# Last attention's loop: the weighted values of a group of tiles issued behind the next group's sums, not in steps between them

## The chip, the cores and the metric

The kernel runs on one core of a Trainium2 chip. The metric is the device time of one execution in microseconds (us); less is better. The engines of the core run side by side, each through its own list of instructions, and meet only at semaphores: TensorE (PE; PEld is its loading of weights), VectorE (DVE), ScalarE (ACT), GpSimd (POOL) and SyncE (SP), which issues the DMAs.

## The reference, cut to what matters

The program is a stack of four layers, each an attention to a context and a feed-forward part, with gated residuals. The change is in the attention of the last layer: 1024 tokens attend to 2048 context rows with 16 heads of width 16. Queries, keys, values and probabilities are rounded to a grid of integers (fake quantization):

```python
q = _fq_sym(q, axis=-1); k = _fq_sym(k, axis=-1); v = _fq_sym(v, axis=2)
attn = jnp.einsum('bhqd,bhkd->bhqk', q, k)
attn = jax.nn.softmax(attn.astype(jnp.float32), axis=-1)
attn = _fq_unsigned(attn, axis=-1)     # s = max / 255; round(attn / s) * s
out = jnp.einsum('bhqk,bhkd->bhqd', attn, v)
```

The largest probability of a row has the exponent 0 after the maximum is taken off, so a rounded probability is the rounded 255 * exp(logit - maximum), and the sum that divides it is that of the exponentials before rounding.

## The kernel before

`layer3_attention` lays out its loop by hand. One head at a time, it needs the maximum of each query's logits before it can form exponentials, so the logits are formed twice: first with the queries on the partitions (`scores`, L2717), from which VectorE takes the maxima (L2891), then with the keys on the partitions and the maximum as three more rows of the contraction (`logits`, L2733), 128 keys by 512 queries in a PSUM bank, of which ScalarE takes the exponentials (L2819, `a_exps`).

The loop runs over steps `s`, 16 for a head (`PER`), and each engine has its own copy of the loop. A step of TensorE issues:

- `scores(s)`: two matmuls, for 128 queries and half the keys. They wait for `ring_free`, that is, for VectorE's maxima of the step before the last: the ring has two places of two banks.
- `logits(m, 0)` and `logits(m, 1)`: the two tiles of pair `m`, `LAG` = 25 steps behind the scores. Each waits until ScalarE has emptied one of three banks.
- work on the exponentials, four steps later (`FILL_LAG`). Four tiles, two pairs, are a group. A chunk is half the queries of a head: 8 steps, numbered `k` = 0 to 7, and 4 groups (`n`, the chunk, and `k` come from `fill_at`). `sums(n, i)` (L2742) adds up the four tiles of group `i` over the keys; it waits for the exponentials. `weighted(n, i)` (L2753) multiplies the rounded tiles by the values; it waits for the rounding of the group's two pairs. Both put their four tiles next to each other into four strips of 32 columns of the array, and into one bank (`OUT`). `sums` reads four-byte exponentials, `weighted` two-byte rounded ones.
- once a head `rows` (L2724), which turns the maxima, and once a head `turn_heads` (L2764), which turns the outcome of a head back.

In the kernel before, sums stand in the steps with odd `k` and the weighted values of groups 0 to 2 in the even step after, between the two logits; those of group 3 come in step 7 behind the second logits.

The rounding of a pair is GpSimd's: L2648 adds a large constant (`a_xn_t` by its older name), L2651 takes it off and writes the two-byte `a_stack`. For every fourth pair, and for all from pair 233 on, VectorE does it in one instruction (L2926, `round_pair`), after the maxima of step `m` + 27. The rounded pairs have six buffers (`PAIRS`), so that a rounding of pair `m` waits for the weighted values of the group that held pair `m` - 6. The exponentials have nine pairs of buffers. GpSimd also splits a head's maxima into three parts (L2656 to L2662), once a head. ScalarE copies the bank `OUT` away after the last group of a chunk (`keep_out`, L2825); the sums of the next chunk wait for that.

No DMA depends on the order of these steps but those of the maxima (L2620), three a head, issued by SyncE.

Of the kernel before, what the change touches and what calls it, by code (L numbers as in the profile page):

```python
# [315 lines left out]
def at_least(eng, sem, value):  # L316

    if isinstance(value, int) and value <= 0:
        return
    eng.wait_ge(sem, value)  # L320
# [2171 lines left out]
def layer3_attention(core):  # L2492
# [10 lines left out]
    with ExitStack() as ctx:  # L2503
# [49 lines left out]
        GROUPS = KT // TILES_PER  # L2553
        STEPS = 2 * GROUPS
# [3 lines left out]
        def fill_at(s):  # L2558

            n, k = divmod(s - LAG - FILL_LAG, STEPS)  # L2560
            return (n, k) if 0 <= n < CHUNKS else (None, None)
# [19 lines left out]
        def rows_slot(s):  # L2581

            h, k = divmod(s - PER - ROWS_LAG, PER)
            return h if k == 0 and 0 <= h < H else None

        def pair_at(s):

            return s - LAG if 0 <= s - LAG < H * PER else None
# [5 lines left out]
        def rounded_by_vector(m):  # L2594

            return sum(by_vector(k) for k in range(m))

        def rounded_by_pool(m):

            return m - rounded_by_vector(m)  # L2600

        with nc.Block() as block:
# [68 lines left out]
            def _(pe):  # L2671
# [39 lines left out]
                def scores(s):  # L2711
                    h, (t, half) = s // PER, divmod(s % PER, 2)
                    n = ring_use["scores", s]
                    if n >= 2:
                        pe.wait_ge(ring_free, n - 1)
                    for c in range(2):
                        mm = pe.matmul(ring(("scores", s))[:, c * BANK:(c + 1) * BANK], qs[0:KS, h * TOK + t * P:h * TOK + (t + 1) * P],  # L2717
                                       ks[0:KS, h * CTX + (2 * half + c) * BANK:h * CTX + (2 * half + c + 1) * BANK], start=True, stop=True)
                    mm.then_inc(ring_full, 1)

                def rows(h):
                    pe.wait_ge(ring_free, ring_use["rows", h] - 1)
                    pe.wait_ge(parts_ready, h + 1)
                    pe.transpose(ring(("rows", h)).bitcast(BF16)[0:3 * NT, 0:P], max_parts[:, h, :, :].rearrange("p s t -> p (s t)"),  # L2724
                                 core.ident_bf[:, :]).then_inc(ring_full, 1)

                def logits(m, u):
                    h, (c, j) = m // PER, divmod(m % PER, KT // 2)
                    if m % PER == 0 and u == 0:
                        pe.wait_ge(ROWS_IN[h % 2], 48 * (h // 2 + 1))  # L2730
                    n, key = 2 * m + u, 2 * j + u
                    at_least(pe, exp_ready, n - LOGIT_BANKS + 1)
                    pe.matmul(core.bank(LOGITS + n % LOGIT_BANKS), ks[0:KM, h * CTX + key * P:h * CTX + (key + 1) * P],  # L2733
                              qs[0:KM, h * TOK + c * QC:h * TOK + (c + 1) * QC], start=True, stop=True).then_inc(logits_full, 1)

                def sums(n, i):
                    g = n * GROUPS + i
                    if i == 0:
                        at_least(pe, out_kept, n)
                    pe.wait_ge(exp_ready, TILES_PER * (g + 1))  # L2740
                    for u in range(TILES_PER):
                        mm = pe.matmul(core.bank(OUT)[32 * u:32 * u + W, :], one_row[:, :], exps[:, (TILES_PER * g + u) % UNITS, :],  # L2742
                                       start=(i == 0), stop=False, skip_group_check=True)
                    mm.then_inc(sums_done, 1)

                def weighted(n, i):
                    g = n * GROUPS + i
                    if g == 0:
                        pe.wait_ge(v_ready, 1)
                    at_least(pe, probs_by_pool, rounded_by_pool(2 * (g + 1)))  # L2750
                    at_least(pe, probs_by_vector, rounded_by_vector(2 * (g + 1)))
                    for u in range(TILES_PER):
                        mm = pe.matmul(core.bank(OUT)[32 * u:32 * u + W, :], v_int[:, TILES_PER * i + u, n // CH, :],  # L2753
                                       probs[:, (2 * g + u // 2) % PAIRS, u % 2 * QC:(u % 2 + 1) * QC],
                                       start=False, stop=(i == GROUPS - 1), skip_group_check=True)
                    mm.then_inc(weighted_done, 1)

                def turn_heads(h):
                    pe.wait_ge(ring_free, ring_use["heads", h] - 1)
                    pe.wait_ge(out_kept, CH * (h + 1))  # L2760
                    tiles = QC // P
                    for c in range(CH):
                        for t in range(tiles):
                            mm = pe.matmul(ring(("heads", h))[:, (c * tiles + t) * W:(c * tiles + t + 1) * W],  # L2764
                                           outs[(CH * h + c) % OUTS][:, t * P:(t + 1) * P], select[:, :], start=True, stop=True)
                    mm.then_inc(ring_full, 1)

                for s in range(SLOT_COUNT):
                    n, k = fill_at(s)
                    if s < H * PER:  # L2770
                        scores(s)
                    if pair_at(s) is not None:
                        logits(pair_at(s), 0)
                    if n is not None and k % 2 == 1:
                        sums(n, k // 2)
                    if n is not None and k % 2 == 0 and k > 0:
                        weighted(n, k // 2 - 1)
                    if pair_at(s) is not None:
                        logits(pair_at(s), 1)
                    if n is not None and k == STEPS - 1:  # L2780
                        weighted(n, GROUPS - 1)
                    if rows_slot(s) is not None:
                        rows(rows_slot(s))
                    if s in TURN_OF:
                        turn_heads(TURN_OF[s])
# [691 lines left out]
```

## Time and profile before

| | |
|---|---|
| median of 3 runs | 3300.67 us (3296.85 to 3310.09) |
| the profiled execution's own time | 3297.79 us |
| its span, first to last instruction | 3296.1 us |
| TensorE busy over the span | 2811.4 us (85%) |
| VectorE / ScalarE / GpSimd busy | 2056.2 / 1520.8 / 828.0 us |
| first exponential of the loop starts | 2418.6 us |
| last exponential of the loop starts | 2865.4 us |

The profiled execution is one of its own, beside the three timed ones. Times in the rows below are microseconds from the start of the span. The loop that is changed fills some 450 us of it. Matmuls are pipelined: the recorded duration of one is longer than the distance to the next, so costs on TensorE are read from start to start.

### The profile page before, as it was taken

To read this page: it belongs to the slowest core of one execution; us is meant where nothing else is said; L and a number is where in the kernel's file an instruction comes from. 1 tells how busy PE (TensorE), PEld (TensorE's weight loads), DVE (VectorE), ACT (ScalarE), POOL (GpSimd) and SP (SyncE) were. 2 spreads that over 40 slices of the span, in tenths; PEclk is the share of its full clock that TensorE was granted. 3 is DMA by queue.
4 is the path that set the end of the run, shared out by engine and by line. 5 is a ranking of instruction groups with operands and counts; after the bars stand their busy time and mean duration, and the time that the engine had idled before them with its cause. 6 is when DMAs were issued, how large, how long until landed. Compare 5 with 4: busy or idle time off the path is not lost. (4 is left out here: it accounts for less than half of the span.)

```text
span 3296.1 us, 47304 instructions
## 1 busy us (share of the span) xinstructions
PE 2811.4 (85%) x15010; PEld 1820.7 (55%) x15010; DVE 2056.2 (62%) x4872; ACT 1520.8 (46%) x3119; POOL 828.0 (25%) x1217
## 2 busy tenths in 40 slices
PE   6887995888899999837999999935689999957898
PEld 4334663777677777615777777724323233334676
DVE  5775336777666666575444444477988888577332
ACT  3452225677666777542222222212347777634221
POOL 0011004444422212010000000031089999402100
PEclk9898997999999999957999999967789999977899
DMA  1002003000000000003000000001000000020000
GB/s 58 1 2 87 1 0 128 14 1 14 14 1 7 8 1 1 1 34 128 1 1 1 0 0 0 0 20 38 8 1 1 1 2 1 1 97 2 1 1 13
DMA packets 37912, 56.98 MB, mean 17 GB/s; under 512 B 6400, under 2 KB 25792, under 8 KB 36416
## 3 DMA queue, kind: packets, MB, share of 16 engines
q1 hardware_dynamic: 37696, 54.35, 4.9%
q8 instruction: 105, 1.72, 0.2%
q14 instruction: 111, 0.91, 0.1%
HBM read 52.99 MB, written 1.05 MB: 16 GB/s over the span
## 5 line engine op out<-in xcount | busy, mean ns | idle before, releaser
L2819 ACT ACTIVATE a_exps<-psum,a_ln 128x512 f32<-128x512 f32 x512 | 333.8, 687 | 147.7 <-PE psum L2733 147.3
L2891 DVE TENSOR_REDUCE a_half_max<-psum 128x1 f32<-128x1024 f32 x256 | 305.2, 1215 | 48.4 <-PE psum L2717 46.6
L1903 DVE TENSOR_REDUCE a_neg_max<-psum 128x2 f32<-128x512 f32 (+1 forms) x128 | 122.5, 957 | 172.0 <-PE psum L1606 169.1
L1556 POOL TENSOR_TENSOR a_head_rstd<-a_head_var,neg_half 128x4 f32<-128x4 f32 x112 | 114.4, 1021 | 394.6 <-DVE a_head_var L1897 214.0
L1626 PE MATMUL psum<-a_probs_t,a_vals 128*128 128x256 f32 x768 | 191.8, 386 | 15.9 <-ACT a_probs_t L1783 15.9
L2651 POOL TENSOR_SCALAR a_stack<-a_xn_t 128x1024 bf16<-128x1024 f32 x175 | 192.9, 1102 | 27.3 <-POOL a_xn_t L2648 26.6
L847 DVE SCALAR_TENSOR_TENSOR f_silu<-f_silu,psum 128x352 f32<-128x352 f32 (+2 forms) x88 | 50.4, 572 | 229.6 <-ACT f_silu L820 229.5
L2648 POOL TENSOR_SCALAR a_xn_t<-a_exps 128x1024 f32<-128x1024 f32 x175 | 191.1, 1092 | 9.1 <-ACT a_exps L2819 9.1
L1606 PE MATMUL psum<-a_k_t,a_q_t 128*128 128x256 f32 (+1 forms) x512 | 190.3, 495 | 0.0
L2733 PE MATMUL psum<-a_qs,a_ks 99*128 99x512 bf16 x512 | 190.0, 387 | 0.1
L1097 DVE TENSOR_REDUCE a_neg_max<-psum 128x2 f32<-128x1024 f32 x64 | 78.4, 1225 | 177.2 <-PE psum L1092 177.2
L2717 PE MATMUL psum<-a_ks,a_qs 96*128 96x512 bf16 x512 | 165.3, 407 | 27.0 <-DVE a_half_max L2891 21.2
L1751 ACT ACTIVATE a_normed<-psum,a_head_bias,a_head_scale 128x128 f32<-128x128 f32 x448 | 168.9, 465 | 40.3 <-POOL a_head_bias L1561 39.3
L1791 ACT ACTIVATE a_probs<-psum,a_neg_max 128x256 f32<-128x256 f32 (+1 forms) x256 | 146.8, 581 | 42.7 <-DVE a_neg_max L1903 42.5
L1626 PEld LDWEIGHTS psum<-a_probs_t,a_vals 128*128 128x128 f32 x768 | 139.8, 191 | 43.4 <-ACT a_probs_t L1783 27.6
L1783 ACT COPY a_probs_t<-psum 128x512 f32<-128x512 f32 x192 | 112.6, 586 | 99.7 <-PE psum L1615 97.4
L1104 ACT ACTIVATE a_probs<-psum,a_neg_max 128x512 f32<-128x512 f32 x128 | 86.7, 682 | 153.3 <-DVE a_neg_max L1097 153.3
L1250 PEld LDWEIGHTS psum<-a_w_v,a_ctx_b 128*128 128x128 f32 x1024 | 124.3, 192 | 31.8 <-issue 30.0
L2733 PEld LDWEIGHTS psum<-a_qs,a_ks 99*128 99x128 bf16 x512 | 48.7, 97 | 164.8 <-ACT a_exps L2819 130.4
L781 PE MATMUL psum<-f_w_silu,f_tile_t 128*128 128x352 f32 (+2 forms) x352 | 136.3, 510 | 3.3 <-issue 2.6
L1638 PE MATMUL psum<-a_w_parts,a_cat 128*128 128x256 f32 x512 | 102.4, 323 | 42.7 <-DVE a_cat L1342 42.7
L805 PE MATMUL psum<-f_w_down,f_hid_t 128*128 128x256 f32 (+1 forms) x576 | 138.7, 380 | 0.0
(485 smaller groups left out, 6415.0 us busy)
## 6 DMA issues: line engine op xcount, KB each, us to landing
a_w_raw<-in_L_xattn_wproj_dram SPq DMA_DIRECT2D x8, 512.0 KB, 3.8
f_w_silu<-in_L_ffn_gate_dram SPq DMA_DIRECT2D x1, 2112.0 KB, 9.3
f_w_mul<-in_L_ffn_up_dram SPq DMA_DIRECT2D x1, 2112.0 KB, 13.9
a_probs<-in_ctx_t_dram SPq DMA_DIRECT2D x4, 512.0 KB, 5.4
f_w_silu<-in_L_ffn_Wu_dram SPq DMA_DIRECT2D x1, 2048.0 KB, 7.9
f_w_mul<-in_L_ffn_Wg_dram SPq DMA_DIRECT2D x1, 2048.0 KB, 12.5
f_w_down<-in_L_ffn_Wd_dram SPq DMA_DIRECT2D x1, 2048.0 KB, 17.5
a_q_raw<-in_L_xattn_wq_dram SPq DMA_DIRECT2D x4, 512.0 KB, 6.8
```

The costliest lines, as they stand in the source:

```text
L781: mm = pe.matmul(core.bank(bank)[:, 0:w], self.tile_t[:, tr, k, :], weights[:, k, first:first + w], start=(k == 0), stop=(k == DK - 1))
L805: mm = pe.matmul(core.bank(6 + tr2)[:, 0:D], self.hid_t[0:w, r, i, :], self.w_down[0:w, base + i, :], start=(c2 == 0 and i == 0), stop=(c2 ...
L1606: mm = pe.matmul(core.bank(SCORES + t)[:, 0:keys], q_t[:, quad % 2, h, t * P:(t + 1) * P], k_t[:, quad % 2, h // 2, 0:keys], start=True, s ...
L1626: mm = pe.matmul(core.bank(OUT)[:, 0:S], vals[:, quad % 2, j, (h // 2) * P:(h // 2 + 1) * P], probs_t[:, g % 2, j, :], start=(j == 0), sto ...
L1751: last = act.activation(normed[:, i % 2, j * P:(j + 1) * P], bank[:, j * P:(j + 1) * P], ACT.Identity, bias=head_bias[:, i % 4, j:j + 1], ...
L1791: last = act.activation(probs[:, g % 2, t, 0:keys], core.bank(SCORES + t)[:, 0:keys], ACT.Exp, bias=neg_max[:, g % 2, t:t + 1], accum_out= ...
L2648: g.tensor_scalar(up, exps[:, first:first + 2, :].rearrange("p u n -> p (u n)"), 1.0, ROUND, ALU.mult, ALU.add).then_inc(lifted_ready, 1)
L2651: g.tensor_scalar(probs[:, m % PAIRS, :], up, -ROUND, 1.0, ALU.add, ALU.mult).then_inc(probs_by_pool, 1)
L2717: mm = pe.matmul(ring(("scores", s))[:, c * BANK:(c + 1) * BANK], qs[0:KS, h * TOK + t * P:h * TOK + (t + 1) * P], ks[0:KS, h * CTX + (2 * ...
L2733: pe.matmul(core.bank(LOGITS + n % LOGIT_BANKS), ks[0:KM, h * CTX + key * P:h * CTX + (key + 1) * P], qs[0:KM, h * TOK + c * QC:h * TOK + ...
L2819: act.activation(exps[:, n % UNITS, :], core.bank(LOGITS + n % LOGIT_BANKS), ACT.Exp, bias=ln255[:, :]).then_inc(exp_ready, 1)
L2891: v.tensor_reduce(half_max[:, h, t, half:half + 1], ring(("scores", s)), AX.X, ALU.max, negate=True).then_inc(ring_free, 1)
```

## The change

Weighted values no longer have steps of their own. Those of group `i` - 1 are issued in the odd step of group `i`, behind its sums and ahead of the second logits; in the last step of a chunk (`k` = 7) those of groups 2 and 3 both follow the sums of group 3, also ahead of the second logits. The loops of the other engines, the waits and the buffers stay.

```diff
                     if n is not None and k % 2 == 1:
                         sums(n, k // 2)
-                    if n is not None and k % 2 == 0 and k > 0:
-                        weighted(n, k // 2 - 1)
+                        if k > 1:
+                            weighted(n, k // 2 - 1)
+                        if k == STEPS - 1:
+                            weighted(n, GROUPS - 1)
                     if pair_at(s) is not None:
                         logits(pair_at(s), 1)
-                    if n is not None and k == STEPS - 1:
-                        weighted(n, GROUPS - 1)
                     if rows_slot(s) is not None:
                         rows(rows_slot(s))
```

## Rows read from the trace of the kernel before

**Rows 1.** Busy time in two stretches: from:to, length, each engine (instructions), clock, DMA.
```profile
2443.00:2837.00 394.00, 384.18 (x2422) 119.18 (x2421) 333.24 (x328) 300.48 (x470) 364.76 (x386) 1.00 0.01 1
2841.00:2866.00 25.00, 24.83 (x173) 7.00 (x175) 13.26 (x21) 23.33 (x39) 0.00 (x0) 1.00 0.00 1
```

**Rows 2.** GpSimd's groups, 2443 to 2837 us: busy, mean ns, idle before.
```profile
L2651 POOL TENSOR_SCALAR a_stack<-a_xn_t 128x1024 bf16<-128x1024 f32 x165 | 182.1, 1104 | 26.2 <-POOL a_xn_t L2648 25.8 <-PE psum L2753 0.3
L2648 POOL TENSOR_SCALAR a_xn_t<-a_exps 128x1024 f32<-128x1024 f32 x165 | 180.2, 1092 | 0.0
```

**Rows 3.** GpSimd's timeline, one instruction of a head and of the next: start, us.
```profile
2603.61 0.19 POOL L2656 CAST a_max_parts<-a_neg_max 128x8 bf16<-128x8 f32 x1
...
2632.31 0.19 POOL L2656 CAST a_max_parts<-a_neg_max 128x8 bf16<-128x8 f32 x1
```

**Rows 4.** Waits of the weight loads, 2443 to 2837 us: total, times, longest.
```profile
PEld psum L2753 <- POOL a_stack L2651: 5.3, 19, 0.4
```

**Rows 5.** Timeline at the end of an even chunk.
```profile
2608.24 1.04 POOL L2651 TENSOR_SCALAR a_stack<-a_xn_t 128x1024 bf16<-128x1024 f32 x1 [0.15 <-POOL a_xn_t L2648]
...
2609.42 0.10 PEld L2753 LDWEIGHTS psum<-a_stack,a_v_int 128*17 128x17 bf16 x4 [0.23 <-POOL a_stack L2651]
```

**Rows 6.** Timeline of two steps of TensorE, and a later rounding of GpSimd.
```profile
2616.32 1.05 PE L2742 MATMUL psum<-a_exps,a_one_row 128*17 128x512 f32 x8
...
2617.30 0.39 PE L2733 MATMUL psum<-a_qs,a_ks 99*128 99x512 bf16 x1
...
2617.53 0.60 PE L2717 MATMUL psum<-a_ks,a_qs 96*128 96x512 bf16 x2
...
2617.97 0.38 PE L2733 MATMUL psum<-a_qs,a_ks 99*128 99x512 bf16 x1
...
2618.28 0.39 PE L2753 MATMUL psum<-a_stack,a_v_int 128*17 128x512 bf16 x4
...
2618.60 0.39 PE L2733 MATMUL psum<-a_qs,a_ks 99*128 99x512 bf16 x1
...
2619.57 1.05 PE L2742 MATMUL psum<-a_exps,a_one_row 128*17 128x512 f32 x8
...
2624.17 1.04 POOL L2651 TENSOR_SCALAR a_stack<-a_xn_t 128x1024 bf16<-128x1024 f32 x1 [0.15 <-POOL a_xn_t L2648]
```

**Rows 7.** Timeline of TensorE at the loop's end, where no logits are left.
```profile
2865.32 0.39 PE L2753 MATMUL psum<-a_stack,a_v_int 128*17 128x512 bf16 x4
...
2865.54 1.03 PE L2742 MATMUL psum<-a_exps,a_one_row 128*17 128x512 f32 x8
...
2866.40 0.39 PE L2753 MATMUL psum<-a_stack,a_v_int 128*17 128x512 bf16 x4
```

**Rows 8.** Timeline in the loop's tail.
```profile
2841.21 8.12 ACT L2819 ACTIVATE a_exps<-psum,a_ln 128x512 f32<-128x512 f32 x13 [0.62 <-PE psum L2733]
...
2841.95 0.10 PEld L2733 LDWEIGHTS psum<-a_qs,a_ks 99*128 99x128 bf16 x1 [0.21 <-ACT a_exps L2819]
...
2843.26 0.11 PEld L2733 LDWEIGHTS psum<-a_qs,a_ks 99*128 99x128 bf16 x2 [0.85 <-ACT a_exps L2819]
```

**Rows 9.** Timeline: two roundings of VectorE and GpSimd's instructions beside them.
```profile
2604.92 1.25 DVE L2926 TENSOR_SCALAR a_stack<-a_exps 128x1024 bf16<-128x1024 f32 x1
...
2605.78 1.28 POOL L2651 TENSOR_SCALAR a_stack<-a_xn_t 128x1024 bf16<-128x1024 f32 x1 [0.15 <-POOL a_xn_t L2648]
...
2627.37 0.68 DVE L2926 TENSOR_SCALAR a_stack<-a_exps 128x1024 bf16<-128x1024 f32 x1
...
2627.39 1.57 POOL L2648 TENSOR_SCALAR a_xn_t<-a_exps 128x1024 f32<-128x1024 f32 x1
```

**Rows 10.** Busy time in two stretches of other parts of the program.
```profile
140.00:160.00 20.00, 18.32 (x102) 7.56 (x102) 13.70 (x35) 10.48 (x11) 0.40 (x1) 0.68 0.00 1
200.00:220.00 20.00, 17.19 (x143) 7.07 (x147) 14.95 (x37) 10.33 (x12) 2.36 (x6) 1.00 0.01 2
```

## The prediction

> **What bounds the loop now.** I read the page for the size of things, then one table of busy time over the loop's steady stretch and its tail, then GpSimd's groups of instructions and the waits of that stretch, and last the timeline of single steps.
>
> The change touches only the loop of the last attention. In 2443 to 2837 us TensorE is busy 384.2 of 394.0 us at a granted clock of 1.00, GpSimd 364.8, VectorE 333.2, ScalarE 300.5 [rows 1]. That looks like a TensorE bound, and the change looks like a gift to it. But busy share does not say which engine waits. GpSimd's two operations for a pair of tiles have 165 runs each, and the only idle time in front of them is 26.2 us in front of L2651, 0.15 us for each pair, put down to GpSimd's own L2648 just before (0.3 us of it to TensorE); in front of L2648 it is 0.0 [rows 2]. So GpSimd never waits for exponentials and never for a free buffer: it is saturated by a dependency chain of its own. Its pace is the loop's: its split of one head's maxima starts at 2603.61 and at 2632.31, 28.70 us apart, and a head is 16 steps [rows 3]. TensorE on its side waits for GpSimd little: 5.3 us in 19 waits of the weight load of the weighted values [rows 4]. At the end of an even chunk (a chunk is half a head's queries, 8 steps) the rounding that the fourth group needs ends at 2608.24 + 1.04 = 2609.28, and its weighted values start at 2609.42 [rows 5]. TensorE is therefore level with GpSimd: 0.14 us later, and it would start to wait. I read this as a loop paced by GpSimd with TensorE hard behind it.
>
> **What the change does to TensorE.** It adds and removes no instruction and no DMA. Weighted values of groups 0 to 2 of a chunk move from the even step to the odd step after it, behind the sums; those of group 3 stay in the last step, but go in front of the second logits.
>
> Prices from single steps [rows 6], start to start; two steps take 3.25 us, 2616.32 to 2619.57. Apart: the first logits of the even step at 2617.97, weighted at 2618.28, second logits at 2618.60, so 0.63 us from logits to logits where the plain spacing is 0.22 (two score matmuls from 2617.53, the logits behind them at 2617.97): the weighted values cost 0.41. Sums to logits is 0.98 (2616.32 to 2617.30). Joined does not occur in the loop's middle, but the loop's end has it, where no logits are left between: weighted to sums is 0.22 (2865.32 to 2865.54), sums to weighted 0.86 (2865.54 to 2866.40) [rows 7]. So sums, weighted, logits takes 0.86 + 0.32 = 1.18 in place of 0.98: 0.20 added. Net 0.41 - 0.20 = 0.21 us saved for each of the 4 x 32 = 128 groups, 27 us of TensorE's time in all. Bounds: 0 if the four-byte sums and the two-byte weighted values change over as dearly as logits and weighted do (0.41), 0.21 by rows 7, the nearest; I take 0.21. The Trainium skill, TensorEngine Tiling (Array Packing), Key Properties, has the reason: a change of the array's tiling mode drains TensorE, while changing between tiles of one mode does not. The rows agree (0.31 and 0.32 against 0.22); by that rule alone two drains in two steps go, and where TensorE sets the pace the time would come down by what they cost.
>
> **What hides it.** I cost the saving at nothing as long as GpSimd sets the pace. About 116 of the 128 groups lie ahead of GpSimd's last pair, 116 x 0.21 = 24 us; uncovered, that would be the gain. Instead TensorE arrives 8 x 0.21 = 1.7 us earlier per head at a rounding that comes no sooner, and the 19 short waits become longer ones.
>
> Behind the new wait stand the second logits and the next scores. ScalarE waits for the logits, VectorE for the scores. Neither is late for GpSimd: when TensorE waits for pair 6 of a chunk, logits up to four or five pairs further have been issued, so GpSimd keeps its supply.
>
> The moved groups also give GpSimd's buffers back one step (1.6 us) later: a rounding needs the weighted values of the group six pairs back. The weighted values at 2618.28 free what the L2651 at 2624.17 writes [rows 6]: 5.9 us early, 4.3 after the change. No stall, so nothing.
>
> **The part that isn't hidden: the tail.** After GpSimd's last pair (it has no instruction in 2841 to 2866 [rows 1]) VectorE rounds alone and there are no scores; ScalarE sets the pace, 13 exponentials in 8.12 us, 0.62 each, back to back [rows 8]. The chain there has no slack that I can see: the first logits of an odd step wait for a bank (2841.95, 0.21 us put down to the exponentials), the second come 1.31 us later, at 2843.26, behind the sums, with 0.39 us to their end, 1.70 in all, while the three logits banks hold 3 x 0.62 = 1.86 us of work for ScalarE, less hand-over [rows 8]. With weighted values between, the 1.31 becomes 1.51 in steps 3 and 5 of a chunk and 1.71 in step 7 (two groups). Chunks 29 and 30 have four such placings each, chunk 31 one before the logits end, and the last step of chunk 28 is delayed by one: 10 x 0.20 = +2.0 us. Bounds: 0 if the banks hide it, 10 x 0.41 = +4.1 if the joint is dear. I take +2.0, by rows 7.
>
> **GpSimd's own pace** can still change. A VectorE rounding that falls beside GpSimd's work stretches it: with one starting at 2604.92, which took 1.25, the L2651 at 2605.78 took 1.28 in place of 1.04; with one at 2627.37, which took 0.68, the L2648 at 2627.39 took 1.57 [rows 9]. So one rounding costs GpSimd 0.24 or 0.53, by where it arrives. Over the stretch that is 165 x (1.104 - 1.044) + 165 x (1.092 - 1.044) = 17.8 us [rows 2], taking 1.044 for an undisturbed run of either (the 1.04 of rows 5). The change moves TensorE and so VectorE's arrivals. Four roundings a head, 394 / 28.70 = 13.7 heads, 55 roundings: between none that costs (-17.8) and all at 0.53 (29.2 - 17.8 = +11.4). Going through one head, most arrivals hang on GpSimd themselves (TensorE waits for it at chunk ends, VectorE finishes behind it), so I take 0 change and keep both ends. The Trainium skill, SBUF — State Buffer, the section on SBUF's two sides, tells of a port pair that VectorE and GpSimd hold as an exclusive lock for a whole instruction. The rows agree in kind; by that rule each rounding could block GpSimd for its whole 0.68, 55 x 0.68 = 37.4, an estimate of +20 us at most, which would be a slower kernel.
>
> **Sum.** Profiled execution 3297.79 us (span 3296.1, so 1.7 around it): 0 for the steady loop, +2.0 for the tail: 3299.8. The median of the three runs, 3300.67, lies 2.9 above the profiled one; so I predict 3303 us.
>
> **Rivals.**
> *A: TensorE is the bound after all.* For it: 97.5% busy, few waits [rows 1, 4]. Against: GpSimd's idle time is all its own [rows 2], and TensorE cannot run ahead of the rounding. It would give 3300.67 - 24 + 2 = 3279. Chance 0.05.
> *B: VectorE's roundings fall otherwise* and change GpSimd's pace, as costed above: 3285 to 3314. Chance 0.18, of which 0.01 beyond either bound of 16.5 us.
> *C (slower): the clock.* TensorE waits more, its busy share falls from 97.5% to some 360 of 394, 91%, in pieces of a us at each chunk's end. In 140 to 160 us, with 18.32 of 20 busy, the granted clock was 0.68; in 200 to 220, with 17.19, it was 1.00 [rows 10]. So a share of 91% decides nothing alone, and the waits would be short. If the clock fell to its lower level (1.2 of 2.4 GHz), a head's 28 us of TensorE would take up to 28 more: from 0.6 of one head in sixteen on, the kernel is slower by over 0.5%; one head gives about 3330. Chance 0.05.
> *D: the joint saves nothing* (0.41, the upper bound): the loop is hidden as well, the tail pays 4.1: 3305. Chance 0.04.
>
> My forecast has 0.68. Within 0.5% (16.5 us, about what a measurement of this kernel tells from no change): 0.68 + 0.16 + 0.04 = 0.88; faster: A and a part of B, 0.06; slower: C and a part of B, 0.06. The range holds the forecast with its tail's bounds (3300.7 to 3304.8), the spread of single runs around their median (-4 to +9), and most of B: 3293 to 3315.
>
> **What would show it.** Right: GpSimd's groups keep their count and have no idle time but their own; its split returns after 28.7 us; waits of weighted values on GpSimd grow from 5.3 to some 20 to 28 us; sums to weighted 0.86, weighted to logits 0.32; in the tail ScalarE's run of 13 breaks up with gaps of 0.2 us. Wrong: a head shorter than 28.4 us (A, or B to the good), longer than 29 (B), a granted clock under 1.00 in the stretch (C), or GpSimd waiting for weighted values (the 4.3 us of cover misjudged).

## The result and the profile after

The changed kernel took 3312.8 us (median of 20 runs), the kernel before 3302.5 in 20 runs of its own: a ratio of 1.0030, 95% interval 1.0022 to 1.0037, some 10 us slower. That is inside the bound of 0.5% and inside the predicted range, but not the +2 us that the sum gave. (One of these twenty runs, at 5793.9 us, and a few of the experiments' were disturbed and are left out of the ratios.)

The loop alone accounts for it: from the first exponential to the start of the last weighted values it took 448.9 us before (2418.6 to 2867.5) and 458.6 after (2422.1 to 2880.7), +9.7. The profiled execution's span is 14.2 longer (3310.3 against 3296.1); 3.5 us of that had passed before the loop and 1.0 come after it, in code that is the same.

What the change does to TensorE is as priced. Two steps of the changed kernel, timeline of TensorE:

```profile
2593.06 1.05 PE L2742 MATMUL psum<-a_exps,a_one_row 128*17 128x512 f32 x8
2593.93 0.40 PE L2753 MATMUL psum<-a_stack,a_v_int 128*17 128x512 bf16 x4
2594.27 0.39 PE L2733 MATMUL psum<-a_qs,a_ks 99*128 99x512 bf16 x1
...
2596.11 1.05 PE L2742 MATMUL psum<-a_exps,a_one_row 128*17 128x512 f32 x8
```

Sums to weighted 0.87, weighted to logits 0.34, and 3.05 us from sums to sums where [rows 6] have 3.25: 0.20 saved for a group. TensorE's busy time in the steady stretch fell from 384.2 us to 370.9. The two stretches of [rows 1] after, then GpSimd's groups of [rows 2]:

```profile
2443.00:2837.00 394.00, 370.93 (x2411) 126.05 (x2413) 320.13 (x326) 288.18 (x467) 364.15 (x377) 0.98 0.01 1
2841.00:2866.00 25.00, 19.75 (x127) 6.28 (x126) 9.55 (x16) 17.35 (x30) 7.63 (x11) 0.86 0.00 1
```
```profile
L2648 POOL TENSOR_SCALAR a_xn_t<-a_exps 128x1024 f32<-128x1024 f32 x163 | 180.1, 1105 | 1.2 <-ACT a_exps L2819 1.2
L2651 POOL TENSOR_SCALAR a_stack<-a_xn_t 128x1024 bf16<-128x1024 f32 x162 | 178.4, 1101 | 25.7 <-POOL a_xn_t L2648 22.6 <-PE psum L2753 2.9
L2656 POOL CAST a_max_parts<-a_neg_max 128x8 bf16<-128x8 f32 x13 | 5.5, 424 | 0.0
```

GpSimd is still saturated: it has one wait of 1.2 us for exponentials, and the 0.15 us ahead of each L2651 remain. (The 2.9 us put down to TensorE are part of those: the weighted values that these roundings needed had started at least 1.8 us before.) But it does 162 and 163 roundings in the time in which it did 165. Its L2648 went from 1092 to 1105 ns in the mean, and the small cast at the head of the split from some 190 to 424. The heads differ now: the split returns after 28.6 and 29.6 us in turn, where it was 28.7 each time. All its 175 roundings took 419.7 us before and 425.9 after, first start to last end. GpSimd's groups over the whole loop (2405 to 2860 us), before, then after; 9.1 us of the idle time ahead of L2648 stand before the first of them:

```profile
L2651 POOL TENSOR_SCALAR a_stack<-a_xn_t 128x1024 bf16<-128x1024 f32 x175 | 192.9, 1102 | 27.3 <-POOL a_xn_t L2648 26.6 <-PE psum L2753 0.3
L2648 POOL TENSOR_SCALAR a_xn_t<-a_exps 128x1024 f32<-128x1024 f32 x175 | 191.1, 1092 | 9.1 <-ACT a_exps L2819 9.1
L2656 POOL CAST a_max_parts<-a_neg_max 128x8 bf16<-128x8 f32 x16 | 3.0, 189 | 0.0
```
```profile
L2648 POOL TENSOR_SCALAR a_xn_t<-a_exps 128x1024 f32<-128x1024 f32 x175 | 193.1, 1104 | 10.3 <-ACT a_exps L2819 10.3
L2651 POOL TENSOR_SCALAR a_stack<-a_xn_t 128x1024 bf16<-128x1024 f32 x175 | 193.0, 1103 | 27.3 <-POOL a_xn_t L2648 23.5 <-PE psum L2753 3.3
L2656 POOL CAST a_max_parts<-a_neg_max 128x8 bf16<-128x8 f32 x16 | 6.1, 380 | 0.0
```

The three were busy 387.0 us before and 392.2 after, +5.2; with the 1.2 of waiting that is 6.4, about the 6.2 that the stretch grew by.

Where TensorE now waits, of the matmuls and of the weight loads, 2443 to 2837 us:

```profile
PE psum L2724 <- POOL a_max_parts L2662: 16.1, 13, 2.8
PE psum L2717 <- DVE a_half_max L2891: 6.6, 11, 0.8
```
```profile
PEld psum L2753 <- POOL a_stack L2651: 18.2, 39, 0.7
```

The waits for roundings grew from 5.3 us [rows 4] to 18.2, close to what was foreseen; the first line of the matmuls is a wait that the prediction didn't have: once a head, `rows` waits for GpSimd's split, up to 2.8 us.

### The profile page after: what moved, and what is told of

The parts are those of the page before. It is cut to its first block and busy times, and to the rows that moved or that the text cites. A ratio compares the mean times of both kernels' runs of the same rounds, so it can differ in the third digit from the quotient of the medians.

```text
span 3310.3 us, 47302 instructions
## 1 busy us (share of the span) xinstructions
PE 2810.9 (85%) x15008; PEld 1833.3 (55%) x15010; DVE 2041.9 (62%) x4872; ACT 1510.8 (46%) x3119; POOL 834.9 (25%) x1217
## 3 DMA queue, kind: packets, MB, share of 16 engines
HBM read 52.99 MB, written 1.05 MB: 16 GB/s over the span
## 5 line engine op out<-in xcount | busy, mean ns | idle before, releaser
L2819 ACT ACTIVATE a_exps<-psum,a_ln 128x512 f32<-128x512 f32 x512 | 323.7, 689 | 167.9 <-PE psum L2733 167.9
L2651 POOL TENSOR_SCALAR a_stack<-a_xn_t 128x1024 bf16<-128x1024 f32 x175 | 193.0, 1103 | 27.3 <-POOL a_xn_t L2648 23.5
L2648 POOL TENSOR_SCALAR a_xn_t<-a_exps 128x1024 f32<-128x1024 f32 x175 | 193.1, 1104 | 10.3 <-ACT a_exps L2819 10.3
L2733 PE MATMUL psum<-a_qs,a_ks 99*128 99x512 bf16 x512 | 176.5, 390 | 3.1 <-ACT a_exps L2819 3.1
L1626 PEld LDWEIGHTS psum<-a_probs_t,a_vals 128*128 128x128 f32 x768 | 139.6, 191 | 44.4 <-ACT a_probs_t L1783 28.7
L2742 PE MATMUL psum<-a_exps,a_one_row 128*17 128x512 f32 x1024 | 140.8, 623 | 0.1
```

The costliest lines, as they stand in the source:

```text
L1626: mm = pe.matmul(core.bank(OUT)[:, 0:S], vals[:, quad % 2, j, (h // 2) * P:(h // 2 + 1) * P], probs_t[:, g % 2, j, :], start=(j == 0), sto ...
L2648: g.tensor_scalar(up, exps[:, first:first + 2, :].rearrange("p u n -> p (u n)"), 1.0, ROUND, ALU.mult, ALU.add).then_inc(lifted_ready, 1)
L2651: g.tensor_scalar(probs[:, m % PAIRS, :], up, -ROUND, 1.0, ALU.add, ALU.mult).then_inc(probs_by_pool, 1)
L2819: act.activation(exps[:, n % UNITS, :], core.bank(LOGITS + n % LOGIT_BANKS), ACT.Exp, bias=ln255[:, :]).then_inc(exp_ready, 1)
```

## The experiments

All ratios are to the kernel before, run on the same chip. The twelve runs stand on three chips, four on each. Times of a loop in parts come from each run's own trace: *stretch*, from the start of GpSimd's first L2648 to the end of its last L2651; *tail*, from there to the start of the last weighted values.

| run | ratio (95%) | stretch us | tail us |
|---|---|---|---|
| before | | 419.7 | 27.9 |
| r_before | 0.9999 (0.9989 to 1.0009) | 419.7 | 29.3 |
| changed | 1.0030 (1.0022 to 1.0037) | 425.9 | 31.4 |
| r_after | 1.0037 (1.0024 to 1.0049) | 425.4 | 30.8 |
| x_tail | 1.0017 (1.0006 to 1.0027) | 425.8 | 29.5 |
| x_rows | 1.0032 (1.0019 to 1.0045) | 427.8 | 34.1 |
| x_k7 | 1.0005 (0.9995 to 1.0014) | 422.8 | 30.5 |
| x_vec_late | 1.0017 (1.0007 to 1.0027) | 425.1 | 34.0 |
| x_vec_early | 0.9997 (0.9988 to 1.0006) | 420.8 | 30.5 |
| x_before_early | 1.0010 (0.9998 to 1.0023) | 420.9 | 29.2 |
| x_before_relief | 0.9993 (0.9983 to 1.0002) | 419.4 | 27.9 |
| x_relief | 0.9956 (0.9942 to 0.9971) | 408.0 | 29.6 |
| x_relief_tail | 0.9952 (0.9939 to 0.9965) | 406.7 | 28.1 |
| x_best | 1.0003 (0.9993 to 1.0013) | 425.2 | 27.6 |

A trace is one execution, a ratio comes from several. The two differ by some us: in `x_vec_late` the loop of the trace is 11.5 us longer than before, and the ratio says 5.6. A few us in one of them alone show little.

**Is it GpSimd that paces?** `x_relief` (on the changed kernel) and `x_before_relief` (on the kernel before) have one edit:

```diff
-            return m % 4 == 3 or m >= H * PER - LAG + 2
+            return m % 4 == 3 or m % PER == 13 or m >= H * PER - LAG + 2
```

> The changed order, with one more pair in sixteen (pair 13 of a head) rounded by VectorE in place of GpSimd. Theory (GpSimd paces): 2.2 us less for GpSimd in each of some 15 heads, while TensorE's own work for a head fell to about 26.3 us: the split returns after 26.5 to 27.5 us in place of 29, and the time falls by 20 to 35 us against the changed kernel, well under before. Rival (TensorE or VectorE pace): within 8 us of the changed kernel.

> The order of before with the same pair given to VectorE. Theory (GpSimd paces, TensorE 0.7 us a head behind it): TensorE becomes the bound at about 28.0 us a head; the time falls by 5 to 12 us against before, so that the changed order with the same relief is faster than this by 10 to 24 us: the hidden gain shows once GpSimd is out of the way. Rival (TensorE paces already): no change within 4 us.

The changed order gained 0.74% of the time from the relief (1.0030 to 0.9956), 24 us, or 19.7 by the loop in the traces; the order of before gained 0.07%, 2 us. Between the two relieved kernels, which shared their runs of before, the join is worth 0.37%, 12 us, or 9.7 by the traces: the gain that it did not show. For the changed order that is what the theory said, with a head of 27.82 us by its splits, a little over the 26.5 to 27.5. For the order of before the number is the rival's, no change within 4 us: a head still takes 28.90 us there, not 28.0. GpSimd's groups, 2443 to 2837 us, first `x_before_relief`, then `x_relief`:

```profile
L2648 POOL TENSOR_SCALAR a_xn_t<-a_exps 128x1024 f32<-128x1024 f32 x151 | 162.8, 1078 | 28.3 <-ACT a_exps L2819 28.3
```
```profile
L2648 POOL TENSOR_SCALAR a_xn_t<-a_exps 128x1024 f32<-128x1024 f32 x150 | 157.3, 1049 | 13.7 <-ACT a_exps L2819 13.7
```

Without its twelfth pair GpSimd waits 28.3 us for exponentials in the order of before: there TensorE, busy 384.1 of the 394 us, is with VectorE the slower one, at about the pace that GpSimd had set. In the kernel before the two were level; the join speeds up one of two.

**The new wait of `rows`.** `x_rows` turns the maxima a step later:

```diff
-        ROWS_LAG, LAG, FILL_LAG = 3, PER + 9, 4
+        ROWS_LAG, LAG, FILL_LAG = 4, PER + 9, 4
```

> The changed order with the turning of a head's maxima (rows) one step later, in step 7 behind the weighted values, which wait for a later rounding than the split. TensorE then never waits for GpSimd's split. Theory (GpSimd paces): the wait only moves to the weighted values of step 7; GpSimd's pace is the roundings' and changes by chance only, within 6 us; 0.998 to 1.002 of the changed kernel. Rival (the new wait for the split and the lower clock after it are what costs): TensorE's clock is 1.00 again in the loop, and the time falls by 5 us or more, to before or under it.

The wait for the split is gone from the list, and TensorE waits as much for roundings instead. Waits of the matmuls and of GpSimd, then busy time in two stretches of `x_rows`:

```profile
PE psum L2753 <- POOL a_stack L2651: 10.2, 8, 1.9
PE psum L2717 <- DVE a_half_max L2891: 5.8, 12, 0.8
```
```profile
POOL a_xn_t L2648 <- ACT a_exps L2819: 5.5, 8, 1.7
```
```profile
2443.00:2837.00 394.00, 377.94 (x2373) 133.32 (x2371) 316.45 (x321) 280.96 (x458) 359.90 (x376) 0.94 0.01 1
2640.00:2650.00 10.00, 9.98 (x45) 4.54 (x45) 5.07 (x7) 4.45 (x8) 9.38 (x9) 0.66 0.00 1
```

By the ratios the time stayed. The clock, which the rival saw back at 1.00, fell further, to 0.94 over the stretch: what TensorE is ahead, it must wait for somewhere. The wait was moved and not taken away, so this run does not price it. Nor was it free in its new place: GpSimd's three instructions take 389.3 us here, 2.9 less than in the changed kernel, but it waits 5.5 us for exponentials, and the stretch is 1.9 us longer.

**The tail.** `x_tail` keeps the order of before from chunk 29 on:

```diff
-                        if k > 1:
+                        if n < 29 and k > 1:
                             weighted(n, k // 2 - 1)
-                        if k == STEPS - 1:
+                        if n < 29 and k == STEPS - 1:
                             weighted(n, GROUPS - 1)
+                    if n is not None and n >= 29 and k % 2 == 0 and k > 0:
+                        weighted(n, k // 2 - 1)
                     if pair_at(s) is not None:
                         logits(pair_at(s), 1)
+                    if n is not None and n >= 29 and k == STEPS - 1:
+                        weighted(n, GROUPS - 1)
```

> The changed order up to chunk 28, the order of before in chunks 29 to 31, after GpSimd's last pair. Theory (tail): ScalarE's chain in the tail pays about 0.2 us for each group placed between the two logits; the exponentials come back to 0.62 each without gaps, and the time falls by about 2 us against the change as it is, to 1.0025 of before. Rival (the tail is slow because TensorE's clock falls at its start): no fall, the tail stays as long as in the changed kernel, 33.7 us from the weighted values of chunk 28's last group to the last of all, against 30.5 before.

The tail came down by 1.9 us (31.4 to 29.5), the stretch stayed (425.8). ScalarE's timeline in the tail, of the changed kernel (chunk 29), then of `x_tail`, where L2823 is the same instruction:

```profile
2852.90 2.42 ACT L2819 ACTIVATE a_exps<-psum,a_ln 128x512 f32<-128x512 f32 x4 [0.62 <-PE psum L2733]
2855.59 2.42 ACT L2819 ACTIVATE a_exps<-psum,a_ln 128x512 f32<-128x512 f32 x4 [0.27 <-PE psum L2733]
2858.28 2.42 ACT L2819 ACTIVATE a_exps<-psum,a_ln 128x512 f32<-128x512 f32 x4 [0.27 <-PE psum L2733]
```
```profile
2855.35 5.64 ACT L2823 ACTIVATE a_exps<-psum,a_ln 128x512 f32<-128x512 f32 x9 [0.26 <-PE psum L2733]
```

Runs of four with a gap, 2.69 us from one to the next, where four back to back take 2.48 [rows 8]: 0.21 for a group between the logits, as worked out. The ratio of `x_tail` is 0.13% lower than that of the changed kernel, 4 us, but the two intervals overlap.

**The last group's place.** `x_k7` puts the last group of a chunk behind the second logits again and leaves the other three joined:

```diff
                         if k > 1:
                             weighted(n, k // 2 - 1)
-                        if k == STEPS - 1:
-                            weighted(n, GROUPS - 1)
                     if pair_at(s) is not None:
                         logits(pair_at(s), 1)
+                    if n is not None and k == STEPS - 1:
+                        weighted(n, GROUPS - 1)
```

> The changed order, but with the last group of a chunk behind the second logits again, as before; groups 0 to 2 stay joined. Theory: in the steady loop this only moves a wait of TensorE, and GpSimd's busy time decides; in the tail two of ten placings are gone, 0.4 to 0.6 us less. Within 5 us of the changed kernel. Rival (the last group's new place, which holds back ScalarE's logits and the copy that the next sums wait for, makes the loss): 8 us or more faster, back to before.

1.0005: a gain of 0.25%, 8 us, by the ratios, back to before as the rival said; by the traces (stretch and tail together) it is 3.9, which is inside the theory's 5. The rows show what else changed. The only wait of the matmuls, then busy time:

```profile
PE psum L2717 <- DVE a_half_max L2891: 25.3, 26, 1.3
```
```profile
2443.00:2837.00 394.00, 368.69 (x2414) 124.87 (x2406) 326.17 (x326) 289.17 (x466) 364.00 (x381) 1.00 0.01 1
```

TensorE no longer waits for the split, it waits for VectorE's maxima, and the clock of the stretch is 1.00 again. L2648, L2651 and L2656 take 389.4 us in place of 392.2, for no cast is stretched (3.1 us for all sixteen). Whether the gain is that of the last group's wait ahead of the logits or of the arrivals of VectorE that follow from it, this run alone doesn't tell.

**When VectorE arrives.** `x_vec_late` and `x_vec_early` move only VectorE's roundings, in the changed order; `x_before_early` does the second in the order of before. The edit of `x_vec_late` (the other two have `s - 1`):

```diff
-                    if pair_at(s - 2) is not None and by_vector(pair_at(s - 2)):
-                        round_pair(pair_at(s - 2))
+                    if pair_at(s - 3) is not None and by_vector(pair_at(s - 3)):
+                        round_pair(pair_at(s - 3))
```

> The changed order with VectorE's roundings one step later, behind the next step's maxima. Nothing else moves. Theory (the loss of the steady loop is GpSimd's stretched instructions): the loop's length between first and last rounding of GpSimd changes by just as much as the busy time of its L2648, L2651 and L2656 together with its idle time (392.2 us busy in the changed kernel, 387.0 before); where VectorE then arrives decides the sign, within -17 to +12 us of the order of before. Rival (order of TensorE's own work costs the time): the time stays at that of the changed kernel within 3 us whatever GpSimd's busy time does.

> The changed order with VectorE's roundings one step earlier, where their exponentials are only just due, so VectorE may wait up to a us there. Theory (GpSimd's stretched instructions): as in the run with them later, the loop changes by GpSimd's busy and idle time, either way. Rival: no change within 3 us, or slower by VectorE's waits alone with GpSimd's busy time as it was.

> The order of before with VectorE's roundings one step earlier. If the earlier roundings helped the changed order only by undoing the arrivals that it had spoilt, there is little left to win here: GpSimd's stretch within 2 us of 419.7, ratio 0.9995 to 1.0005. Rival (earlier roundings are better by themselves): 4 us or more faster than before.

GpSimd's groups over the whole loop of `x_vec_early`:

```profile
L2651 POOL TENSOR_SCALAR a_stack<-a_xn_t 128x1024 bf16<-128x1024 f32 x175 | 195.1, 1115 | 27.3 <-POOL a_xn_t L2648 24.6 <-PE psum L2753 2.3
L2648 POOL TENSOR_SCALAR a_xn_t<-a_exps 128x1024 f32<-128x1024 f32 x175 | 189.1, 1081 | 9.1 <-ACT a_exps L2819 9.1
L2658 POOL TENSOR_TENSOR a_max_rest<-a_neg_max,a_max_parts 128x8 f32<-128x8 f32 x16 | 4.2, 265 | 1.4
L2656 POOL CAST a_max_parts<-a_neg_max 128x8 bf16<-128x8 f32 x16 | 3.0, 187 | 0.0
```

With the roundings a step earlier GpSimd's three instructions take 387.2 us (392.2 in the changed kernel), and it waits for exponentials only ahead of its first rounding. Its stretch is 420.8, still 1.1 over before, of which L2658, the second instruction of the split, has 1.0 (4.2 us for 3.2). The ratio is 0.9997, 11 us under the changed kernel (6 by the traces). TensorE's order is the same, so most of the loss of the steady loop lies not in that order by itself but in the arrivals that came with it. A step later the three take 392.2 again (L2648 longer, L2656 shorter) and the stretch is 425.1, as in the changed kernel, so that run could not tell theory from rival. In the order of before, earlier roundings win nothing (387.7 and 420.9): they are not better by themselves.

What an arrival costs, in the timeline of the changed kernel (GpSimd's and VectorE's rows), in one head and in the next:

```profile
2610.20 0.68 DVE L2926 TENSOR_SCALAR a_stack<-a_exps 128x1024 bf16<-128x1024 f32 x1
2610.23 0.70 POOL L2656 CAST a_max_parts<-a_neg_max 128x8 bf16<-128x8 f32 x1
...
2638.31 0.68 DVE L2926 TENSOR_SCALAR a_stack<-a_exps 128x1024 bf16<-128x1024 f32 x1
...
2639.84 0.19 POOL L2656 CAST a_max_parts<-a_neg_max 128x8 bf16<-128x8 f32 x1
```

A cast of 128 x 8 elements that takes 0.19 us [rows 3] takes 0.70 beside a rounding of VectorE's that got in 0.03 us ahead of it. In the kernel before this never happened (all 16 casts of the loop took 184 to 190 ns, with VectorE's rounding mostly 1.31 us behind them); after the change six of the sixteen are stretched, one in two heads, and the sixteen take 6.1 us in place of 3.0. No semaphore stands between the two instructions: the engines do not meet at semaphores alone. It is the same with the roundings: in the traces of both kernels no L2648 or L2651 without a rounding of VectorE's beside it took more than 1.05 us, and each of those that took 0.1 us more than 1.04 (59 of 350 before, 54 after) had one.

**The same program again.** `r_before` and `r_after` repeat both kernels:

> The kernel before, once more, for its trace on this chip beside the others. GpSimd's stretch from the first to the last rounding should return at 419.7 us and the tail at 27.9, within 1 us, if its pattern is settled by the program; a ratio of 1 within 0.1% shows what the comparison can tell. Rival (the pattern of arrivals differs from execution to execution): the stretch differs by 3 us or more.

> The changed kernel, once more, on the same chip. If the pattern is settled by the program: GpSimd's stretch 425.9 us, the tail 31.4, ratio 1.003. Rival (chance of one execution): a stretch that differs by 3 us or more, with the ratio anywhere between 1.000 and 1.004.

The stretches return within 0.6 us (419.7 and 419.7; 425.9 and 425.4), the changed kernel with six stretched casts both times: the pattern of arrivals belongs to the program, not to the execution. The tails vary by 0.6 to 1.4: in `r_before` the clock was 0.83 at the tail's start (2840 to 2850 us), in before 1.00.

**Put together.** `x_relief_tail` is `x_relief` with the edit of `x_tail`; `x_best` has the earlier roundings besides.

> The changed order with pair 13 of each head given to VectorE, and the order of before in chunks 29 to 31. If both parts add up: 2 us under the changed order with the relief alone, 0.995 of before. If the tail's cost was tied to the lower clock there, no better than the relief alone.

> The changed order, pair 13 of each head given to VectorE, the order of before in chunks 29 to 31, and VectorE's roundings one step earlier: all that helped, together. If they add: 0.993 to 0.995 of before. Rival (with GpSimd relieved, TensorE waits for VectorE's maxima, and VectorE's earlier roundings make those later): no better than 0.9952, or worse.

`x_relief_tail` is the fastest, 0.9952; its tail is 1.5 us shorter than that of `x_relief`, which the ratios can't tell apart. `x_best` was a miss: 1.0003. In 2443 to 2837 us GpSimd waits 33.5 us for exponentials there (12.6 in `x_relief_tail`), TensorE's matmuls 23.8 for VectorE's maxima (17.2), and the clock is 0.97 (1.00). An edit that helped a loop paced by GpSimd hurts this one, in which GpSimd has time to spare. That fits the rival, that the earlier roundings hold up VectorE's maxima, but no run separates them from the lower clock.

## Why the prediction came out as it did

**The bound: right, half told.** GpSimd sets the pace of the changed order, as the relief shows, and TensorE's 24 us stayed hidden; with the relief 12 of them came out. That TensorE was hard behind was read from 0.14 us of slack; `x_before_relief` shows how hard: relieved of GpSimd, that order is no faster, so the two were level. Rival A, TensorE as the only bound, falls: the saving on TensorE brought no gain.

**The prices on TensorE: right.** 0.20 saved per group for the 0.21 forecast, read from the loop's end, where the joint could already be seen.

**The tail: right in its cause, short in size.** +2.0 forecast, 1.9 given back by `x_tail`, and 1.5 between `x_relief` and `x_relief_tail`, whose tails both ran at a clock of 1.00. In all the tail grew by 3.5 (27.9 to 31.4), or 1.5 between the repeats (29.3 to 30.8). Where the rest comes from was not tested. Just ahead of the tail, which starts at 2849.33, TensorE waits 3.43 us for the last split, and its clock is 0.66 in the 10 us around; in the tail itself it is 0.99. So the tail may begin with TensorE late. Busy time, and the timeline of that place:

```profile
2840.00:2850.00 10.00, 6.57 (x38) 2.27 (x30) 1.94 (x4) 4.36 (x8) 8.63 (x11) 0.66 0.00 1
```
```profile
2844.55 0.27 PE L2724 MATMUL psum<-ident_bf,a_max_parts 128*24 128x128 bf16 x1 [3.43 <-POOL a_max_parts L2662]
...
2845.28 1.91 PE L2742 MATMUL psum<-a_exps,a_one_row 128*17 128x512 f32 x8
```

**The step that was mis-sized: "so I take 0 change and keep both ends" for GpSimd's own pace.** It was +5.2 us of busy time and 1.2 of waiting, and the stretch grew by 6.2, the largest part of the 9.7 and inside the ends that were kept (-17.8 to +11.4). The reason given, that most arrivals hang on GpSimd, did not hold at the split: before, VectorE's rounding starts 1.31 us after the first cast, and after the change 0.02 us or 1.53 us ahead of it, head by head in turn. Only in the second of these three places the cast is held up; in the others the two do not overlap. And of GpSimd's instructions only the roundings were priced; the split's small cast, which costs 0.5 us when VectorE gets in just ahead of it, was not: +3.1 of the 5.2. What came in is therefore rival B, which had a chance of 0.18, and its sign, a head longer than 29 us, stands in every second head (29.6). That 3312.8 lies in the range is owed to the ends that were kept for B, not to the sum: that said 3303.

**Where TensorE would wait: half right.** The weighted values' wait came out a little under what was said (18.2 us for 20 to 28); that `rows` stands one step earlier and waits for the split was overlooked. It cost little by itself: `x_vec_early` still has 11.4 us of it, and a clock of 0.98 in the steady stretch, with GpSimd's stretch only 1.1 us over before. But it gathers the idle time in one piece.

**Rival C: its first half happened.** The clock left 1.00 in the steady loop. Timeline of the changed kernel where `rows` waits for the split, then busy time just after:

```profile
2640.99 0.22 PE L2724 MATMUL psum<-ident_bf,a_max_parts 128*24 128x128 bf16 x1 [1.60 <-POOL a_max_parts L2662]
```
```profile
2640.00:2650.00 10.00, 9.01 (x55) 3.71 (x56) 4.92 (x8) 4.34 (x8) 9.15 (x13) 0.83 0.00 1
```

The same wait of 1.60 us stands at 2582.80, 2699.19 and 2757.50, one of 2.79 at 2524.58, each with a fall behind it, for some us, to the lower level of 1.2 GHz; at 2495.23 and 2815.70 it has none. The price was not the "up to 28 more" of a head: GpSimd, not TensorE, set the pace, and slower matmuls ate waiting time. What can be left of it is the 1.2 us that GpSimd waited once, at 2445.87 after such a stretch, and some of the tail. In `x_rows`, at 0.94, GpSimd did begin to wait: 5.5 us.

**Open.** How much of the gain of `x_k7` comes from the last group's place and how much from the arrivals that follow was not separated, nor was what makes `x_best` slow, nor what the tail lost beyond the groups between its logits. Nor was a loop without any VectorE rounding beside GpSimd tried, which would give the whole price of these meetings.

## What to carry to other kernels

Busy shares of 97% and 93% side by side do not say which engine paces; idle time with its releaser does, and an engine whose only waits are on itself does. When two engines are level, making one faster gains nothing, and the way to see the gain is to relieve the other in the same run and compare. In a loop as regular as this one, the moment at which two engines hold each other up is part of the schedule: price every instruction that can be met, small ones too, and expect a reorder elsewhere to move it. Here that was 6 us, 0.2% of the kernel.

## What the hardware showed

A VectorE rounding, 0.68 us where nothing holds it up, stretched GpSimd's 0.19 us cast to 0.70, and its 1.04 us roundings by 0.24 or 0.53 [rows 9]. That is less than the whole 0.68 each that the Trainium skill, SBUF — State Buffer, in the section on SBUF's two sides, would allow at most. VectorE is held up as well: a rounding took 1.25 where it started at 2604.92, 0.33 us behind a GpSimd instruction of 1.04 us [rows 9]. A matmul of four column strips that follows another with other element types costs no changeover (0.22 from weighted to sums, [rows 7]; 0.87 for the four of sums, then weighted). Going from full-width matmuls to strips and back cost some 0.2 us for both ways (0.31 and 0.32 where 0.22 is plain, [rows 6]). That agrees with the drain of which the Trainium skill, TensorEngine Tiling (Array Packing), Key Properties, tells; it gives no price.
